# A mixture-of-experts tower on one core: six early tiles woven into the last rounds, and a tile table with a tile per partition

## The reference, cut to what matters

```python
h = _L0_tok_ref(x, W, b, gamma, beta)              # 128 x 124 x 256
h = h + attention(layernorm(h), ...)               # keys and queries of 256
rh = relu(features @ router_w1 + router_b1)        # features = layernorm(h)
top_w, top_i = top_k(softmax(rh @ router_w2 + router_b2), 2)
routing_weights = softmax(top_w)
h1 = relu(features @ expert_w1[e] + expert_b1[e])
h2 = relu(h1 @ expert_w2[e] + expert_b2[e])
out = h + sum over the two experts of (h2 @ expert_w3[e] + expert_b3[e]) * routing_weights
```

## Time and profile before

| | us |
|---|---|
| median of 3 runs | 1345.66 |
| lowest and highest | 1345.20, 1346.94 |
| profiled execution | 1342.78 |
| its span, first to last instruction | 1341.0 |
| TensorE busy | 1234.8 (92%) |
| VectorE busy | 1062.5 (79%) |
| GpSimd busy | 928.3 (69%) |
| ScalarE busy | 838.0 (62%) |

### The profile page before, as it was taken

The page is one execution under the profiler, slowest core; times in us unless marked ns, Lnnn a source line. Parts: engine busy times, 40 slices in busy tenths (PEclk is TensorE's granted clock), DMA queues, the critical chain, the costliest instruction groups (busy, mean ns, idle before and its releaser), DMA issues. The chain is left out here.

```text
span 1341.0 us, 28426 instructions
## 1 busy us (share of the span) xinstructions
PE 1234.8 (92%) x7888; PEld 1078.0 (80%) x7888; DVE 1062.5 (79%) x3590; ACT 838.0 (62%) x1838; POOL 928.3 (69%) x740
## 2 busy tenths in 40 slices
PE   3899999999999999999629999999999999999994
PEld 3788888888888888887428788888888888888883
DVE  3589989998999899987547778787787787777873
ACT  1477666766676667766316666766667667666662
POOL 2127778777877787777753677676676676766766
PEclk7899999999999999999759999999999999999997
DMA  2124555544444444445677796667876778778755
GB/s 83 31 63 130 147 131 150 142 115 113 117 124 116 114 116 124 116 114 161 174 204 198 159 225 113 123 122 146 193 120 113 126 154 178 129 146 191 122 63 60
DMA packets 134564, 176.50 MB, mean 132 GB/s; under 512 B 38019, under 2 KB 102406, under 8 KB 134406
## 3 DMA queue, kind: packets, MB, share of 16 engines
q0 software_dynamic: 75456, 69.19, 32.7%
q1 hardware_dynamic: 56822, 101.44, 24.8%
q10 hardware_dynamic: 2128, 4.05, 1.0%
HBM read 168.72 MB, written 101.48 MB: 202 GB/s over the span
## 5 line engine op out<-in xcount | busy, mean ns | idle before, releaser
L533 POOL DMA_INDIRECT out<-yo,tail x268 | 438.7, 1637 | 199.3 <-issue 147.7
L481 POOL DMA_INDIRECT expert_rows<-rec,row_i x256 | 347.6, 1358 | 78.4 <-issue 64.2
L909 ACT ACTIVATE h2v<-bank,small 128x512 f32<-128x512 f32 x134 | 92.4, 690 | 206.9 <-PE bank L725 191.9
L749 PE MATMUL bank<-w_sb,h_hi 128*128 128x256 f32 x1072 | 208.7, 288 | 2.0 <-issue 2.0
L725 PE MATMUL bank<-x_hi,w_sb 128*128 128x512 f32 x536 | 178.2, 393 | 6.3 <-issue 2.7
L725 PE MATMUL bank<-h_hi,w_sb 128*128 128x512 f32 x536 | 177.0, 391 | 1.2 <-DVE h_lo L1229 1.2
L749 PEld LDWEIGHTS bank<-w_sb,h_hi 128*128 128x128 f32 x1072 | 171.3, 191 | 2.8 <-issue 2.7
L749 PE MATMUL bank<-w_sb,h_lo 128*128 128x256 f32 x536 | 151.4, 283 | 0.0
L868 ACT ACTIVATE xn<-h,nmr,rstd 124x256 f32<-124x256 f32 x128 | 66.4, 589 | 126.0 <-DVE nmr L1082 126.0
L725 PEld LDWEIGHTS bank<-x_hi,w_sb 128*128 128x128 f32 x536 | 101.3, 189 | 30.3 <-issue 7.3
L469 POOL TENSOR_TENSOR rstd<-vareps,neghalf 124x4 f32<-124x4 f32 x96 | 114.5, 1192 | 8.0
(11 more groups left out here) (187 smaller groups left out, 3115.0 us busy)
## 6 DMA issues: line engine op xcount, KB each, us to landing
w_sb<-split_weights SPq DMA_DIRECT2D x201, 512.0 KB
xg<-expert_rows SPq DMA_DIRECT2D x67, 530.0 KB
out<-h SPq DMA_DIRECT2D x32, 496.0 KB
small<-in_esmall SPq DMA_DIRECT2D x69, 134.0 KB
split_weights<-half_w SPq DMA_DIRECT2D x36, 256.0 KB
x_in<-in_x SPq DMA_DIRECT2D x32, 250.0 KB
raw_w<-in_eweights SPq DMA_DIRECT2D x36, 128.0 KB
out<-yo,tail POOLq DMA_INDIRECT x268
```

Of the source, the lines that this page charges most:

```text
L481: pool.indirect_dma_start(rows_dram, bass.IndirectOffsetOnAxis(ap=row_i[0:TOK, slot, j, k:k + 1], axis=0), rec[0:TOK, slot, j, :], None).t ...
L533: pool.indirect_dma_start(out, bass.IndirectOffsetOnAxis(ap=tail[:, s, j, E8:].bitcast(I32), axis=0), yo[:, ys, j, :], None, compute_op=AL ...
L749: mm = pe.matmul(banks[6 + b][:, (j % 2) * D:(j % 2 + 1) * D], act[:, c, j * P:(j + 1) * P], w[:, 2, c, wh, :], start=(c == 0 and p == 0), ...
L909: act.activation(h2v[:, m, :], banks[4 + m][:], ACT.Relu, bias=small[:, slot, DC + m:DC + m + 1]).then_inc(S["h2_v"], 1)
```

## The change

Tiles 0 to 5 no longer come from the table. After group 19 VectorE picks the expert with the most rows so far (`choose_early`, 14 instructions in round 23), which by then has at least six full tiles. SyncE loads its weights in rounds 28 and 29 and the rows of tiles 0 to 3 in rounds 30 and 31, which need only the scatters of groups 0 to 19. The turn and the first and second layer of tile 0 and the turn and first layer of tile 1 are written into rounds 33 to 35 (`DRAIN = 33`) on PE, ScalarE and VectorE; they use banks 6, 7, 1 and 2, which the rounds no longer need there. The other tiles follow in the order of before, without the six. With these inputs the early expert is number 3; tile 6 is then of expert 0.

The table is made with a tile on each partition (10 operations in the step of tile 1, 9 in that of tile 2), goes to DRAM and comes back as one row on one partition. Chunks of weights are split three at a time in rounds 0 to 3, then one at a time, and are done in round 27. SyncE writes the pad rows instead of ScalarE; the last scatter waits for nothing, and the rows of tile 6 wait for the pads instead. `yo` has four buffers and `tail` eight.

```diff
+EARLY = 6
+DECIDE = 19
+FIRST_CHUNKS = 4
+YO = 4
+TAILS = 8
+DRAIN = G + 1
...
+        def chunks_of(it):
+
+            if it < FIRST_CHUNKS:
+                return range(3 * it, 3 * it + 3)
+            n = it + 2 * FIRST_CHUNKS
+            return range(n, min(n + 1, NCHUNK))
...
+                if DRAIN - 5 <= it < DRAIN - 5 + WSLOTS:
+                    early_weights(it - (DRAIN - 5))
+                if DRAIN - 3 <= it < DRAIN - 1:
+                    t = 2 * (it - (DRAIN - 3))
+                    early_rows(t)
+                    early_rows(t + 1)
...
+            for t in range(SLOTS, EARLY):
+                next_rows(t)
+            sp.wait_ge(S["table"], PADS_AT)
+            for e in range(NE):
+                at = sp.value_load(pad_at[0:1, e:e + 1], min_val=0, max_val=NE * REGION)
+                sp.dma_start(rows_dram[bass.ds(at, TILE), :].rearrange("(p j) n -> p (j n)", p=P),
+                             pad_rows[:].rearrange("p j n -> p (j n)")).then_inc(S["pads_written"], 16)
+            for t in range(SLOTS, EARLY):
+                wait_apart(sp, S["y_dve"], (t - SLOTS + 1) * 4, S["sp_passed"])
+                load_small(t)
+            sp.wait_ge(S["table"], TABLE_AT)
+            sp.dma_start(tab_dram, t_coli[0:NT, :]).then_inc(S["tab_kept"], 16)
+            sp.wait_ge(S["tab_kept"], 16)
+            sp.dma_start(tab[:], tab_dram.rearrange("(o t) k -> o (t k)", o=1)).then_inc(S["tab_loaded"], 16)
+            sp.wait_ge(S["tab_loaded"], 16)
+            for i in range(SENT):
+                sp.wait_ge(scattered[i], sent_to(i, G))
+            sp.wait_ge(S["pads_written"], 16 * NE)
+            next_rows(EARLY)
...
-                    if g == G - 1 and n == GB * TOPK - 1:
-
-                        pool.wait_ge(S["pads_written"], 16 * NE)
...
+            def add_tile(t):
+
+                wait(pool, y_added[t % 2], landed(t - 2))
+                if t < EARLY:
+                    wait(pool, y_added[(t - 1) % 2], landed(t - 3))
...
+                if it == DRAIN:
+                    pe.wait_ge(S["v_ready"], G * 2)
+                    turn(0, 6)
...
+                if it == DRAIN + 1:
+                    first_layer(0, 6)
+                if it == DRAIN + 2:
+                    first_layer(1, 6)
...
+                if it == DRAIN + 1:
+                    pe.wait_ge(S["av"], G * AV_N)
+                    turn(1, 1)
+                    pe.wait_ge(S["xn2T_sb"], G * 2)
+                    pe.wait_ge(S["rh_sb"], G)
+                    second_layer(0)
...
+            for t in range(1, NT):
+                split(t, h1v, h1_hi, h1_lo, S["h1_v"], S["h1_split"])
                 if t + 1 < NT:
...
+                    rows_low(t + 1)
+                rows_out(t - 1)
+                split(t, h2v, h2_hi, h2_lo, S["h2_v"], S["h2_split"])
+                if t == 1:
+                    tile_table_rows()
+                if t == 2:
+                    tile_table_experts()
+            rows_out(NT - 1)
```

More of the change, by code:

```diff
@@ L299, in _ @@
             const(rb1_col[:], rb1)
-            load_chunk(0, 0, 0)
+            for n in range(RING):
+                load_chunk(n)
             def spare_rows(i):
@@ L761, in _ @@
+            pipeline(step)
+            pe.wait_ge(S["topk"], (G - 1) * TOPK_N + 1)
+            turn(2, 0)
+            third_layer(0)
+            second_layer(1)
+            pe.wait_ge(S["pos"], (G - 1) * POS_N + 1)
+            for t in range(2, NT):
+                first_layer(t, 2)
+                if t + 1 < NT:
+                    turn(t + 1, 0)
+                third_layer(t - 1)
+                second_layer(t)
+            third_layer(NT - 1)
         @block.scalar
@@ L877, in step, with read_rows @@
                                        ACT.Identity).then_inc(S["v_ready"], 1)
-            pipeline(step)
-            write_pads(act, range(NE))
-            def read_rows(t):
+                if it == DRAIN:
+                    read_rows(0, 6)
+            def read_rows(t, at):
                 for c in range(DC):
@@ L918, in _, with first_values @@
-            read_rows(0)
-            tiles(tile_step)
+            def first_values(t, bank):
+                act.wait_ge(small_loaded[t % SLOTS], t // SLOTS * 16 + 16)
+                for m in range(DC):
+                    act.wait_ge(S["h1_ps"], t * 2 + m + 1)
+                    wait(act, S["h1_split"], t * 4 - 2 + 2 * m)
+                    act.activation(h1v[:, m, :], banks[bank + m][:], ACT.Relu,
+                                   bias=small[:, t % SLOTS, m:m + 1]).then_inc(S["h1_v"], 1)
@@ L921, in _ @@
+            pipeline(step)
+            for t in range(1, NT):
+                first_values(t, 6 if t == 1 else 2)
+                if t + 1 < NT:
+                    read_rows(t + 1, 0)
+                second_values(t)
+                gate_rows(t - 1)
+            gate_rows(NT - 1)
         @block.vector
```

538 lines of the change are left out of this document (263 added, 275 removed).

## The result

The changed kernel takes 1304.89 us (median of 4, 1304.3 to 1305.36) against 1345.43 of the kernel before (median of 4, 1343.24 to 1346.94). The ratio is 0.9699 with a 95% interval of 0.9687 to 0.971, so the change is 3.0% faster. The profiled execution took 1304.3 us with a span of 1302.5, 38.5 less than the span of before; the other 2 us are how the two profiled executions lie to their medians.

The account below looks back on a forecast made before the run. The seam was taken as bound by GpSimd's scatter queue and the last groups' data. Terms 28 + 3.8 - 3.5 + 1.2 - 2 = 27.5 us less than the profiled 1342.78, 1315.3, or 1318 as median; range 1309 to 1330.

Parts of the forecast that it names:

- the seam: Stretch between the program's two halves, rounds 33 to 35 through the turn of tile 5: 28 us gained, 20 to 31.
- the walk of tiles 1 to 4: VectorE sets the pace, 7.8 us a tile plus 3.0 and 2.7 for the table; tile 5's transposes at 706.
- The handovers: Waits between engines that a step-by-step walk leaves out: 3 us taken off its 30.9 us gain, leaving 28.
- Behind the seam: Tiles 5 to 8: more `tail` and `yo` buffers remove VectorE's wait for adds, 3.8 us gained, 0 to 4.5.
- The choice of the expert: Round 23 on VectorE: 14 small operations on the path at 0.25 us each, 3.5 us lost (0.20 to 0.30 each).
- The chunks: Eight weight chunks moved from rounds 28 to 35 to rounds 0 to 3: 1.2 us gained, 0 to 1.4.
- The early loads: Weights and rows loaded on SyncE in rounds 28 to 31, ahead of the next x_in: costed at nothing.
- Tile 6: SyncE's long queue with the table's write and read back delays the rows of tile 6: 2 us lost, 0 to 8.
- Nothing slips: Rival for the whole change: the walk is exact and no load is late, 34 us gained, 1312; chance 0.15.
- The low clock: Rival in the seam: PE's clock stays low between short waits, seam 10 us longer, 1328; chance 0.16.
- The late table: Rival at tile 6: a DMA trip takes 10 us instead of 4.3, tile 6 some 13 us late, 1331; chance 0.10.
- turn of tile 5 near 711: Sign at the end of the seam: transposes of tile 5 on PE near 711 us in the new trace.

Follow-up runs that it names:

- the second execution of the changed kernel: The changed kernel run once more with nothing altered, as base for the follow-ups: 1304.88 us, ratio 0.9699 to the kernel before.
- the later run of the table: Changed kernel with the table made once more in the step of tile 3 (19 more small operations, results not read): 1305.16 us.
- the run without the weave: Changed kernel with early rows kept, but every step of tiles 0 and 1 placed behind round 35: 1318.65 us, ratio 0.9792 to the kernel before.
- the longer queue: Changed kernel with a second table write and read back on SyncE ahead of the rows of tile 6: 1310.11 us, ratio 0.9742 to the kernel before.
- five kernels in which PE's waits lay otherwise: Changed kernel with tile 0's rows read earlier in round 33, in five variants: 1310.91, 1312.04, 1311.37, 1306.27 and 1306.13 us.
- the run with two tables: Changed kernel with the table made twice in the steps of tiles 1 and 2, copies not read: 1309.06 us, ratio 0.9721 to the kernel before.
- three experiments here: Changed kernel with tile 0's rows read earlier in round 33 and `tail` moved ahead of `xv`, three variants: 1310.91, 1312.04 and 1311.37 us.

## Why the prediction was wrong

**The sign and the mechanism were right, the seam was mis-sized.** Of the 11.0 us by which the gain in the traces (38.5) exceeds the 27.5 forecast, 7.4 lie in the seam, 2.0 at tile 6, 1.1 in the head and 0.5 in the rest. The seam was put at 28 us and measured 35.4 (33.0 in the second execution of the changed kernel). The step that failed is the walk of tiles 1 to 4 and the 3 us taken off it. In the clock of before (the new trace less 1.2 us) the first layers of tiles 2, 3 and 4 start at 679.2, 689.5 and 698.7 and the turn of tile 5 at 701.4; the walk had 681, 692, 703 and 706. So 4.6 us of the miss are the walk's and 2.9 the handovers'. Of the 4.6, 1.3 lie ahead of tile 1, 0.5 and 0.7 in the next two steps, 1.8 in the step of tile 3 (9.2 us where the walk had 11) and 0.3 behind it. By the walk's own prices the last two steps were 10.8 and 10.5 us (7.8 and the table), so 0.7 us are its rounding.
- *VectorE's price.* A tile was 7.8 us of VectorE by summed durations. From the first split of tile 3 to that of tile 4 the queue of the changed kernel (694.41 to 702.99) takes 8.6 us with 1.2 of waits in it, so 7.4 of work: durations of neighbours overlap. The table was 3.0 and 2.7 us by the price of the old one and took 2.0 (682.83 to 684.85) and 1.3 (693.13 to 694.41). That this is because it is 124 rows of 8 and no longer one row of 536 is argued, not tested.
- *Who sets the pace.* The walk let VectorE set every step, 11 us for the last two. Only the steps up to the turns of tiles 3 and 4 (10.40 and 10.28) are VectorE's, by its backlog from round 35, and in the second some 1.1 us of it are casts and subtractions that ran slower than their kind; the later run of the table cost half its time because from tile 4 on PE sets the pace with 9.2.
- *The handovers.* Nothing was left out: from the turn of tile 1 on, waits of 0.6 to 0.9 us on PE are all the seam shows, and they lie inside the steps above.
- *The rest of the walk.* PE could start the first layer of tile 1 at 668.3 in the clock of before (669.46), the walk had 669.6: 1.3 of the 4.6 us.

**Behind the seam** 3.8 us came as forecast (27.64 instead of 31.43). In the old order the buffers alone give 3.9 by ratio, but only 2.2 of it in this stretch, so the agreement of the two numbers is in part luck. What the prediction did not see is that the new order could not live without them: with the old ones it loses 11.4 us.

**The choice of the expert** cost 2.64 us in its round instead of 3.5: 0.19 us an operation, just under the 0.20 to 0.30 allowed.

**The chunks** were to give 1.2 us. The head lost 1.2 us in all by round 33, with 0.3 already lost before round 23 and 2.6 in it, so 1.8 came back after it. As a price for VectorE the term holds: a round without a chunk takes 18.8 us (`xT_lo` at 547.06 and 565.88), one with it 19.1, so 0.3 each. But one chunk a round, as before, costs 10.5 us in the new order, most of it by what stands behind the last ones in SyncE's queue. A step that moves a transfer was costed on the engine that prepares it and not on the queue that issues it, though the prediction lists that queue item by item under tile 6.

**The early loads** were put at nothing. In the first execution they cost nothing in the end: VectorE waits 1.13 us at 585.92 for `xT_hi`, which waits for `x_in` behind three weight loads, and has it back a round later. In the run with the old buffers it waits 1.30 and 2.49 us there, and the two rounds take 40.6 us instead of 37.6. The kernel before and the run with one chunk a round show no such wait. So this term is 0 to 3 us by the execution, and the cover of a round that the prediction gave it is not always enough.

**Tile 6** was to lose 2 us and lost none. The two trips took 10.6 us instead of 8.6, but the table was ready at 694.5 instead of 698 (699 in the new clock), so the rows were issued at 705.1 and not at 709.7 (708.5 plus 1.2); they needed 3.7 us to land. The margin was 3 us. Two things were off inside the sum. The 1.7 us for the register read had no row; from the end of the last wait to the issue it took 1.3 (703.8 to 705.08). And the wait for the last scatters was put at nothing, though it, and not the read back, ended last, here and in eleven more of the seventeen executions with the woven order. So in this one a faster table would not have brought the rows forward. The margin was partly luck too: the write took 4.4 to 10.4 us in the seventeen. Three of them, with SyncE's queue as in the changed kernel, had 9.4, 9.4 and 10.4, and their step from tile 6 to tile 7 was 0.6 to 2.1 us longer, in the last with a wait of 1.78 us for weights. The page "DMA: Bandwidth & Descriptors" of the Trainium skill (Anatomy of one DMA) gives some 2 us fixed for a DMA, in a section on those that GpSimd issues; these are SyncE's. The runs agree in two places only: 1.92 us for the write in the run without the weave, where the last pad had been issued 12.7 us before, and 2.40 for the second write of the longer queue.

**The rivals.** "Nothing slips" (1312) was the nearest and still too slow, since it kept the walk's prices. The low clock hardly came to the changed kernel (0.97, and 0.90 in its second execution), but it is real: 0.50 to 0.61 from 660 to 670 us in five kernels in which PE's waits lay otherwise, and it cost 1.4 us in the run with two tables. The page "TensorE: Matmul & The Clock Gate" of the Trainium skill (HAM oscillation) has a stream with repeated waits start each burst slow; here the first layer behind the 3.8 us wait did start slowly, and the clock was back within some 4 and 7 us in the two executions of the changed kernel; in the other order, with a wait of 1.9 to 2.6 us in another place, it stayed low for 10 to 13 us. Which detail of the order decides that stays open. The late table came when its queue was lengthened, and late writes by chance cost up to 2.1 us. The signs "turn of tile 5 near 711" (702.6 in the new trace) and "a round of 22 us" (21.74) show the two cases side by side: one mis-sized walk, one good term.

**The range** reached down to 1309, only 3 us below the walk's own best case (1312). The prices common to all cases (7.8 us a tile, 0.30 us an operation of the table) were never given a lower end.

## What to carry to other kernels

In a hand walk of two engines take, step by step, the larger of their paces, price an engine's work by start-to-start times of the same rows and not by summed durations, and let the range cover an error of that price, since every rival shares it. Cost a moved step on each queue it leaves and enters: here the chunks were costed at 1 us of VectorE, and one that SyncE must wait for held up everything behind it, most of 10 us. List the waits beside a transfer as well: in the end the rows of tile 6 waited for the last scatters and not for the table. The worth of a buffer belongs to an order of work: the same buffers are worth 4 us in one order and 11 in the other, so measure it again when the order changes.

## What the runs showed of the hardware

- Operands shifted by 128 bytes (or 1152) against the weights in SBUF make the 128x512 product 395 ns instead of 390 and the run 6 us (0.45%) longer; by 256 bytes they do not. Whether the remainder by 256 bytes is the rule, three shifts suggest and do not prove; whether it is the distance to the weights or the operands' own address, they do not tell, since the weights stayed where they were. Anything allocated ahead of such tensors can do this by accident, as it did to three experiments here.
- A write of 1.3 KB to DRAM and the wait for it took 4.4 to 10.4 us in seventeen executions of the woven order, 1.9 us in the run without the weave and 2.4 us when it followed another such write and its read back. In the seventeen, six pad writes and two small loads stood ahead in the queue, but with the same queue it took 5.8, 6.6, 9.4 and 10.4 us, so the queue does not explain the spread.
- The granted clock fell to 0.50 behind a wait of PE of only 2.39 us (the run with two tables, 692 to 694 us). In the second execution of the changed kernel it was 0.50 again from 668 to 670 us, behind waits of 0.77 and 0.58 us; in the first it stayed at 1.00 there, behind waits of 0.77 and 0.59.
- From 681 to 693 us casts of 128x512 on VectorE take up to 0.90 us instead of 0.42. Pad writes and GpSimd's scatters run beside them or just before; neither was taken away. In the run with the chunks as before, two such casts at 667.0 and 668.4 us took 0.69 and 0.90 us, 19 us ahead of its first pad write, so pads are not needed for it. The cause is open.
